# A level-embedding, attention and ternary feed-forward block: two bias loads moved to another queue, the table normalised ahead of the tokens, and the output rows copied by both engines in turn

## What is computed

```python
def step(lvl, d):
    lvl = jnp.clip(lvl + d, 0, num_levels - 1)
    return (lvl, lvl)
...
h = level_emb[levels] * SCALE                       # SCALE = 0.15
h = h + attn(_layernorm(h))                         # 16 query heads, 4 key/value heads, head size 16
h = h + ffn(_layernorm(h))

def _quantize(W):
    gamma = jnp.mean(jnp.abs(W))
    return jnp.clip(jnp.round(W / (gamma + EPS)), -1.0, 1.0)
h = jax.nn.relu(jnp.einsum('bsd,fd->bsf', x, Wq1) + b1)      # 256 -> 1024
out = jnp.einsum('bsf,df->bsd', h, Wq2) + b2                 # 1024 -> 256
```

## Time and profile before

| | before |
|---|---|
| median of 3 runs | 55.86 us (53.93, 55.86, 55.99) |
| the profiled execution's own time | 54.04 us |
| its span in the trace | 52.0 us |
| granted TensorE clock over the span | 0.995 |
| TensorE busy | 88% |
| VectorE busy | 73% |
| ScalarE busy | 66% |
| GpSimd busy | 30% |
| transfer queues | 5.37 MB moved, of it 2.10 MB written |

### The profile page before, as it was taken

How to read it: one execution, slowest core, us unless ns; L and a number is a source line. 1 busy time by engine, 2 the same in 40 slices (tenths; PEclk the granted TensorE clock), 3 DMA queues, 4 the chain that set the end, 5 groups by cost and what they waited for, 6 DMA issues and landing times.

```text
span 52.0 us, 1206 instructions
## 1 busy us (share of the span) xinstructions
PE 45.6 (88%) x394; PEld 36.3 (70%) x394; DVE 38.0 (73%) x141; ACT 34.2 (66%) x77; POOL 15.7 (30%) x37
## 2 busy tenths in 40 slices
PE   0999999999999799999999999999999999993000
PEld 0336469894758688768679999989999798860000
DVE  3558994698985289999999996269858889659100
ACT  0083231380799997989988999999967793509000
POOL 5689952000005950009200579970000000000000
PEclk9999999999999999999999999999999999999997
DMA  0183919999753100000000000000000005555893
GB/s 0 36 234 77 44 63 350 410 432 368 198 124 98 47 7 0 0 0 0 0 0 13 0 0 0 0 6 0 0 0 0 0 13 200 203 208 195 295 385 127
DMA packets 4658, 5.37 MB, mean 103 GB/s; under 512 B 1117, under 2 KB 4141, under 8 KB 4653
## 3 DMA queue, kind: packets, MB, share of 16 engines
q1 hardware_dynamic: 4312, 5.02, 31.2%
q10 hardware_dynamic: 341, 0.29, 1.6%
HBM read 3.21 MB, written 2.10 MB: 102 GB/s over the span
## 4 chain that ended last, share of the span: by engine, by line
PE 76%; DVE 10%; POOL 3%; issue 1%; ACT 1%; DVEq 1%
PE pswt L1258 16%; PE psmisc L1273 15%; PE psg L1067 8%; PE psg L1063 5%; PE psg L1194 4%; POOL rs L445 3%; PE psg L1240 3%; DVE aw L952 2%; PE psg L1106 2%; PE psg L1153 2%; PE psg L1203 2%; PE psg L1154 2%; PE psg L1158 2%; DVE cn L892 2%; DVE hq L906 2%; DVE st L910 2%
## 5 line engine op out<-in xcount | busy, mean ns | idle before, releaser
L587 ACT ACTIVATE hr<-pswt,b1c 128x256 f32<-128x256 f32 x16 | 7.6, 484 | 1.2 <-PE pswt L1258 0.9
L1273 PE MATMUL psmisc<-w2T,hh 128*128 128x256 f32 x32 | 8.2, 285 | 0.0
L1273 PE MATMUL psmisc<-w2T,hl 128*128 128x256 f32 x32 | 8.1, 281 | 0.0
L937 DVE TENSOR_TENSOR hl<-hr,hh 128x256 fp32r<-128x256 f32 x16 | 6.7, 435 | 1.2 <-ACT hh L589 0.9
L1258 PE MATMUL pswt<-xhi,w1T 128*128 128x256 f32 x32 | 7.0, 299 | 0.0
L1258 PE MATMUL pswt<-xlo,w1T 128*128 128x256 f32 x32 | 6.4, 280 | 0.0
L1273 PEld LDWEIGHTS psmisc<-w2T,hh 128*128 128x128 f32 x32 | 6.0, 189 | 0.1
L1273 PEld LDWEIGHTS psmisc<-w2T,hl 128*128 128x128 f32 x32 | 6.0, 189 | 0.0
L445 POOL TENSOR_TENSOR rs<-ve,mhalf 128x1 f32<-128x1 f32 x4 | 2.7, 686 | 9.1 <-DVE ve L918 9.1
L440 POOL TENSOR_TENSOR voc<-vo,cpos 128x272 f32<-128x272 f32 x4 | 2.7, 714 | 8.1 <-DVE cpos L858 8.1
L1258 PEld LDWEIGHTS pswt<-xhi,w1T 128*128 128x128 f32 x32 | 4.9, 189 | 0.3
(11 more groups left out here) (177 smaller groups left out, 108.4 us busy)
## 6 DMA issues: line engine op xcount, KB each, us to landing
w<-in_L_ffn_W_dram SPq DMA_DIRECT2D x4, 512.0 KB, 6.8
out_dram<-aw SPq DMA_DIRECT2D x7, 256.0 KB, 2.4
wq<-in_L_attn_Wq_dram SPq DMA_DIRECT2D x1, 256.0 KB, 3.5
wo<-in_L_attn_Wo_dram SPq DMA_DIRECT2D x4, 64.0 KB
out_dram<-aw ACTq DMA_DIRECT2D x1, 256.0 KB, 2.9
emb<-in_L_tok_level_emb_dram SPq DMA_DIRECT2D x1, 128.0 KB
bo_bc<-in_L_attn_bo_dram SPq DMA_DIRECT2D x1, 128.0 KB, 8.8
b_bc<-in_L_ffn_b_dram SPq DMA_DIRECT2D x1, 128.0 KB, 7.3
```

Of the source, the lines that this page charges most:

```text
L587: nc.scalar.activation(hr[:, n % NHR, :], pswt[n % 2][:, 0:RH], ACT.Relu, bias=b1c[:, j:j + 1]).then_inc(a_hr, 1)
L937: V.tensor_tensor(hl[:, n, :], hr[:, n % NHR, :], hh[:, n, :].bitcast(F32), ALU.subtract).then_inc(v_hl, 1)
L1273: ins = mm(psmisc[r][:, 0:D], part[:, n, r * P:(r + 1) * P], w2T[:, j, :], start=(j == 0 and m == 0), stop=(j == FC - 1 and m == 1))
```

## The change

Four things are edited.

1. `bvr` and `bkc` are issued by ScalarE instead of SyncE, behind `bq2`; on SyncE the four FFN loads follow Wv directly. The tokens are issued as three plain transfers of 16 x 128 instead of one with a repeated source, and `open_tokens` waits for all three (`d_tok` at 48).
2. The orders of all four computing engines are written anew. DVE does `norm_table` ahead of `open_tokens`; TensorE does `table_t` ahead of `drops`. Further on steps change places, of which three stand in the rows below.
3. Output rows: ACT copies sequences 0 and 2 of a group, DVE 1 and 3, each copy raises its own semaphore count, and each store waits for one copy of either engine.
4. `table_load()` (an activation on one element) moves from the front of ScalarE's list to the place ahead of `last_store()`. The instruction that loads the activation tables stays one, ahead of ScalarE's first activation.

```diff
             sp.dma_start(wv[:], Wv.rearrange("(c p) n -> p c n", p=P)).then_inc(d_wv, 16)
-            sp.dma_start(bvr[:], bv.unsqueeze(0)).then_inc(d_bv, 16)
-            sp.dma_start(bkc[:], bk.unsqueeze(0).unsqueeze(2).to_broadcast([2, KVD, 1])).then_inc(d_bk, 16)
             for i in range(2):
...
-                if g < NG - 1:
-                    sp.wait_ge(a_out, g + 1)
-                    sp.dma_start(out_t[:, b0:b0 + 2, :], osb[:, g, 0:2, :]).then_inc(d_out, 16)
-                sp.wait_ge(v_out, g + 1)
-                sp.dma_start(out_t[:, b0 + 2:b0 + 4, :], osb[:, g, 2:4, :]).then_inc(d_out, 16)
+                for e in range(2):
+                    if g == NG - 1 and e == 0:
+                        continue
+                    b0 = g * BG + 2 * e
+                    sp.wait_ge(a_out, 2 * g + e + 1)
+                    sp.wait_ge(v_out, 2 * g + e + 1)
+                    sp.dma_start(out_t[:, b0:b0 + 2, :], osb[:, g, 2 * e:2 * e + 2, :]).then_inc(d_out, 16)
...
+            residual(0)
             inverse_root(0)
...
-            act.dma_start(tok3[:], x.unsqueeze(0).to_broadcast([3, B, S])).then_inc(d_tok, 16)
+            for i in range(3):
+                act.dma_start(tok3[B * i:B * i + B, :], x).then_inc(d_tok, 16)
             act.dma_start(bq2[:], bq.rearrange("(k a e d) -> a e k d", k=KV, a=2, e=2)).then_inc(d_bq, 16)
+            act.dma_start(bvr[:], bv.unsqueeze(0)).then_inc(d_bv, 16)
+            act.dma_start(bkc[:], bk.unsqueeze(0).unsqueeze(2).to_broadcast([2, KVD, 1])).then_inc(d_bk, 16)
...
             def last_store():
-                act.wait_ge(a_out, NG)
+                act.wait_ge(a_out, 2 * NG - 1)
+                act.wait_ge(v_out, 2 * NG - 1)
...
             def result(g):
-                for b in range(2):
+                for b in range(0, BG, 2):
                     act.wait_ge(p_out, g * BG + b + 1)
-                    ins = nc.scalar.activation(osb[:, g, b, :], out_banks(g)[b][:, 0:D], ACT.Copy)
-                ins.then_inc(a_out, 1)
+                    nc.scalar.activation(osb[:, g, b, :], out_banks(g)[b][:, 0:D], ACT.Copy).then_inc(a_out, 1)
...
             result(3)
+            table_load()
             last_store()
...
-                for b in range(2, BG):
+                for b in range(1, BG, 2):
                     dve.wait_ge(p_out, g * BG + b + 1)
-                    ins = V.tensor_copy(osb[:, g, b, :], out_banks(g)[b][:, 0:D])
-                ins.then_inc(v_out, 1)
+                    V.tensor_copy(osb[:, g, b, :], out_banks(g)[b][:, 0:D]).then_inc(v_out, 1)
...
             threshold(0)
+            threshold(1)
...
             inverse_sums(2)
+            ternary(0)
+            ternary(1)
             normalise(2)
...
             keep_warm(8, psg[0])
...
             less_max()
-            keep_warm(3, psmisc[0])
             abs_total(0)
+            abs_total(1)
             context(0)
```

More of the change, by code:

```diff
@@ L481, in _ @@
             scaled_mean(3)
-            residual(0)
             residual(1)
@@ L605, in _ @@
             magnitudes(0, 0)
+            magnitudes(0, 1)
+            magnitudes(1, 0)
             prefix_out()
-            magnitudes(0, 1)
             max_hi()
-            magnitudes(1, 0)
             magnitudes(1, 1)
@@ L613, in _ @@
             exps(2)
+            exps(3)
             rounded(0)
@@ L616, in _ @@
             ctx_out(1)
-            exps(3)
+            ternary(0)
             rounded(1)
-            ternary(0)
             ctx_out(2)
@@ L986, in _ @@
             top_onehot()
+            level_onehot(0)
             signs(0)
-            level_onehot(0)
             level_onehot(1)
+            count_blocks()
+            identities()
             max_parts()
-            count_blocks()
+            signs(1)
             counts_out()
-            signs(1)
             threshold(0)
+            threshold(1)
             inverse_sums(0)
@@ L998, in _ @@
             normalise(1)
+            table_bias()
             inverse_sums(2)
+            ternary(0)
+            ternary(1)
             normalise(2)
-            table_bias()
-            threshold(1)
-            ternary(0)
             add_table(0)
+            inverse_sums(3)
             row_stats(0)
@@ L1008, in _ @@
             row_stats(1)
-            inverse_sums(3)
             variance_eps(0)
+            normalise(3)
             row_moments(1)
-            normalise(3)
             variance_eps(1)
-            ternary(1)
             norm_rows(0)
+            add_table(2)
             norm_rows(1)
             ternary(2)
-            ternary(3)
             x_lo(0)
             x_lo(1)
-            add_table(2)
+            ternary(3)
+            row_stats(2)
             add_table(3)
-            row_stats(2)
+            hidden_lo(0, 0)
             row_stats(3)
             row_moments(2)
+            row_moments(3)
             variance_eps(2)
-            hidden_lo(0, 0)
-            row_moments(3)
             variance_eps(3)
@@ L1039, in _ @@
             hidden_lo(1, 0)
+            final(0)
             hidden_lo(1, 1)
             hidden_lo(1, 2)
-            final(0)
+            final_lo(0)
             hidden_lo(1, 3)
+            hidden_lo(1, 4)
             final(1)
-            final_lo(0)
-            hidden_lo(1, 4)
+            hidden_lo(1, 5)
             result(0)
-            hidden_lo(1, 5)
             final_lo(1)
@@ L1288, in spread @@
                 for b in range(BG):
-                    if 1 <= g < NG - 1 and b % 2 == 0:
-                        pe.wait_ge((a_out, v_out)[b // 2], g)
+                    if 1 <= g < NG - 1:
+                        pe.wait_ge((a_out, v_out)[b % 2], 2 * (g - 1) + b // 2 + 1)
                     q = slice(L * b, L * (b + 1))
@@ L1301, in _ @@
             warm_up(6, psg[0])
-            keep_warm(8, psg[0])
+            keep_warm(9, psg[0])
+            table_t()
+            keep_warm(4, psg[0])
             drops()
-            keep_warm(5, psg[0])
-            table_t()
-            keep_warm(6, psg[0])
+            keep_warm(2, psg[0])
+            query_bias()
             keys()
-            query_bias()
             queries()
-            keep_warm(5, psg[0])
+            keep_warm(10, psg[0])
+            levels_out()
             values()
@@ L1313, in _ @@
             scores_t(0)
-            levels_out()
             level_ends()
+            scores_t(1)
             prefix_t()
-            scores_t(1)
+            scores_t(2)
             maxima()
-            scores_t(2)
             scores_t(3)
@@ L1329, in _ @@
             context_t(1)
-            abs_total(1)
+            context(3)
             out_proj(0)
             out_proj(1)
-            context(3)
             context_t(2)
+            keep_warm(1, psmisc[0])
             weights_t(0)
@@ L1338, in _ @@
             context_t(3)
+            keep_warm(2, psmisc[0])
+            weights_t(2)
             rows_t(0)
             rows_t(1)
-            weights_t(2)
+            weights_t(3)
             out_proj(3)
-            weights_t(3)
+            ffn1(0, 0)
+            ffn1(0, 1)
             weights_t(4)
             weights_t(5)
-            ffn1(0, 0)
-            ffn1(0, 1)
-            weights_t(6)
             ffn1(0, 2)
@@ L1358, in _ @@
             ffn1(0, 6)
+            weights_t(6)
             weights_t(7)
```

83 lines of the change are left out of this document (40 added, 43 removed).

## The result

| | before | after |
|---|---|---|
| device time, median of 4 runs | 54.89 us (53.26 to 55.99) | 61.13 us (60.13 to 62.53) |
| the profiled execution's span | 52.0 us | 60.5 us |
| granted TensorE clock over the span | 0.995 | 0.898 |
| TensorE busy | 45.6 us, 88% | 49.0 us, 81% |

The ratio is 1.130 [1.084, 1.176]: slower, by 6.2 us between the medians, and outside the range of 53.3 to 56.7 us that was given.

The account below looks back on a forecast made before the run. The prediction took the kernel for a TensorE queue full most of its time. Its terms +0.1 + 0.0 - 0.3 + 0.3 + 0.2 - 0.2 gave +0.1 on the profiled 54.04 us; median forecast 55.8 us, range 53.3 to 56.7.

Parts of the forecast that it names:

- Loads: Start of the kernel: ScalarE's six transfers stay hidden by 0.7 us; SyncE reaches W1 1.3 us earlier; no bandwidth gained.
- The base of 55.9 us: Starting time for the median forecast: two of three runs shown lay at 55.9 us, one at 53.93.
- Table before tokens: Front up to less_max: TensorE never waits, the earlier table gains nothing, less_max ends at 16.5 instead of 16.41; +0.1 us.
- From less_max to the contexts: Exponentials start 0.4 us earlier, but signs ahead of cpos delay voc, so context(0) starts at 17.6 against 17.57; 0.0.
- abs_total(1), -0.3: After the contexts on TensorE: abs_total(1), 0.34 us, moves into the wait for context(0); -0.3 us.
- 20.13 to the feed-forward: Three matmuls on zeros behind context_t(2) and (3) cost +0.3 us; VectorE's later second row block makes rows_t(1) wait, +0.2.
- Feed-forward: From 28 us on: same matmuls in another order without a gap, 0.0, up to +0.4 for VectorE's backlog.
- output: Last copies and stores: one copy on each engine starts the store 0.2 us earlier and the end follows; -0.2 us.
- the gap closes: Faster rival, behind less_max: context(0) starts at 17.1, -1.2 us in all, median 54.65; chance 0.15.
- The clock: Rival at the front: the 1.2 GHz clock could rise at another moment, either way; held in the range, no separate chance.
- ScalarE starts late: Slower rival, loads: each token transfer costs 1.33 us to issue, queries end late, +1.1 to +1.2 us, median 57.0; chance 0.07.
- VectorE or POOL becomes the bound between 20 and 31 us: Slower rival: lateness of 0.6 at rows_t(1) and 0.5 in the first hidden_lo, +1.1 us, median 57.0; chance 0.12.

Follow-up runs that it names:

- e2: The kernel before with only bkc moved to ScalarE's queue, behind bq2: 58.73 us, ratio 1.093 to the kernel before.
- e16: e1 with counts_out ahead of signs(1) and without the three matmuls on zeros behind context_t(2) and (3): 52.82 us, ratio 0.987 to the kernel before.
- e12: The kernel before with only the changed kernel's engine orders and place of the one-element activation; loads, tokens and output copies as before: 53.31 us, ratio 0.998.
- e1: The changed kernel with bkc put back on SyncE's queue, behind Wv and ahead of W1: 52.86 us, ratio 0.979 to the kernel before.
- e7: e1 with five instead of ten matmuls on zeros behind the queries: 52.95 us, ratio 0.987 to the kernel before.
- e13: e1 with abs_total(1) and W2's threshold back behind context_t(1): 53.47 us, ratio 0.991 to the kernel before.
- e14: e1 without the three matmuls on zeros behind context_t(2) and context_t(3): 53.01 us, ratio 0.986 to the kernel before.
- e5: e1 with the output rows copied and stored as in the kernel before: 53.18 us, ratio 0.990 to the kernel before.
- e3: The changed kernel with bkc as ScalarE's first transfer, ahead of the tokens: 60.99 us (59.48 to 62.21).
- e11: The changed kernel, bkc still last on ScalarE's queue, but SyncE waits for its landing before issuing W1: 54.21 us, ratio 1.015 to the kernel before.
- e4: The changed kernel with 52 more matmuls on zeros between values and scores: 58.87 us, ratio 1.099 to the kernel before.
- e15: The changed kernel with the key bias loaded at the same place as a two-piece row, added by a TensorE matmul: 61.82 us, ratio 1.143 to the kernel before.
- e18: The changed kernel with bkc's 128 pieces as two transfers whose outermost dimension is 64: 58.96 us, ratio 1.102 to the kernel before.
- e10: e1 with both signs and identities() on VectorE moved behind max_parts() and counts_out(): 53.58 us, ratio 1.000 to the kernel before.
- e6: e1 with counts_out ahead of signs(1) on VectorE: 52.98 us, ratio 0.986 to the kernel before.

## Why the prediction was wrong

*Loads: the step that failed.* The prediction counted for every moved transfer what it costs to issue and when the issuing engine is free again. That part held as a whole: the three tokens were issued in 1.38 us, the table load ended at 5.54 (5.4 forecast; `bq` cost 1.23 us to issue instead of 0.68, `bvr` 0.24 instead of 0.61), the transpose stood at 5.76 (5.85), the queries ended at 9.5 (9.25). It never asked when a moved transfer lands and who waits for it: the landing of `bkc` stood at nothing in the sum, without a reason. Before, `bkc` was issued at 3.54 and `ktm` started at 8.57 without waiting for it. Now it went from ahead of W1 to beside W1 and landed at 14.97, and `klo`, the scores' last input, which the walk had ready by about 10.95, was done at 17.47. "TensorE never waits up to less_max" became a wait of 5.76 us, and less_max ended at 25.63 instead of 16.5. The rule that the prediction cites from the Trainium skill (DMA: Bandwidth & Descriptors, "Issuing engines are not separate DMA queues"), that issuers share the 16 engines, was read as "no gain"; here it was a warning too. SyncE's earlier W1 (issued at 2.65 instead of 4.21), booked as the gain, may make it worse: 11.3 us of landing against 8.6 in e2, where W1 was issued at 3.59, behind `bkc` and not ahead of it; no run isolates this. No rival had this mechanism: the two slow ones were of issue time and of a computing engine.

*The base of 55.9 us.* The forecast of a median took the upper level for the usual one, from two of three runs. Of the 96 later runs of the kernel before only 16 lie there.

*Table before tokens, +0.1.* The walk of the front was right in its parts up to 9.5 us, within 0.3. Its end, less_max at 16.5, was reached where `bkc` was in time: 16.57 in e16, 16.28 in e12. But "TensorE never waits up to less_max" is not quite so even there: VectorE's `ms` is on the chain in e1, `oh` and `sg` too in e16, and with five matmuls on zeros also `klo` (e7).

*From less_max to the contexts, 0.0, and abs_total(1), -0.3.* The exponentials came as early as forecast (0.05 us behind less_max's end in e1, 0.52 before). But `cpos` was over at 15.42 in e1, 0.04 ahead of less_max's end, not 0.1 behind it, GpSimd's first product started 0.11 behind it, not 0.25, and a product took 0.61 us, not 0.69. The first context starts 0.9 to 1.0 us behind less_max (1.16 before) and TensorE has no gap after it. Both terms together measured -0.6 (e13: 30.91 against 30.32), twice their sum.

*20.13 to the feed-forward, +0.3 and +0.2.* Both 0.0. The three zeros cost nothing (e14, without them: 30.33). `rows_t(1)` doesn't wait in e1; it does in e13, for 0.21.

*Feed-forward 0.0, output -0.2.* Right: no gap, and the end follows the last matmul by 4.5 instead of 4.7 us; e5, with the old copies, has 4.7 and a median 0.3 us above e1's, which the noise could make too.

With `bkc` in time the sum would have been 0.1 - 0.6 - 0.2 = -0.7 on the profiled time. The rival *the gap closes* is the mechanism that e1 shows behind less_max, at half its price. *The clock* was held in the width of the range as a moment of rising; that it can fall again in a wait, which cost 1.7 to 3 us here, was not thought of. *ScalarE starts late* and *VectorE or POOL becomes the bound between 20 and 31 us* didn't happen.

## What to carry to other kernels

When a load is moved to another queue, write down for it not only the issue but the landing: what is under way at that time on the other queue, and which step waits for it. Small transfers that a step needs early go ahead of the bulk, on whatever queue; whichever stand last on the second queue when the bulk starts are late, and putting another one last (e3) only changes who waits. A wait on TensorE's path is to be priced twice: its length, and the clock that may fall in it. The second can be the larger price: in e3, waits of 2.6 us went with a less_max 9.9 us later.

## What the runs showed of the hardware

- 128 pieces of 4 bytes landed 2.8 us after issue with no bulk beside them (e11) and 8.6 to 11.3 us beside SyncE's loads, of which W1 and W2 are 2 MB (e2, e4, the changed kernel); two pieces of 256 bytes took 5.7 us (e15), the 128 as two transfers of 64 took 7.5 from the second's issue and 8.0 from the first's (e18). In the changed kernel, between 7 and 9 us, ScalarE's queue (q10) got 8 packets through while SyncE's (q1) got 225:

```profile
q1 hardware_dynamic: 225, 0.81, 102.1%
q10 hardware_dynamic: 8, 0.00, 0.2%
```

- GpSimd and VectorE slowed each other where a sign of 128x1024 lay beside products of 128x272 (e10): 1.10 us for each sign instead of 0.65, 0.83 for each product instead of 0.61. In e6, with one sign beside them, the four products took 2.74.
- The clock fell in an idle stretch of TensorE of 5.8 us (the changed kernel, whose four runs have mean clocks of 0.90 to 0.94), and also in e3, in the second of two waits of 1.3 us, and in e15, in one of 1.7 us. In e18 it fell while TensorE was at work, 1.6 us after a wait of 0.2. It stayed up in e4, where the wait of the changed kernel was filled with matmuls on zeros. In e3, e15 and e18 it then stayed at 1.2 GHz for 10 to 14 us. What the kernel before does in the 16 of 96 runs with the lower mean clock is open.
